# Reading the eight remainder rows of an adjacency matrix in halves, sixteen lanes instead of eight

## What is computed

```python
neighbors = adj @ h                                  # 5000 x 5000 times 5000 x 64
neighbors = neighbors / (num_neighbors[:, None] + 1e-7)
out = concatenate([h, neighbors], axis=-1) @ fc_w.T + fc_b
return x + relu(out)
```

## Time and profile before

| | |
|---|---|
| median of 3 runs | 246.63 us (246.61 to 246.72) |
| the profiled execution: its time, its span | 246.69 us, 245.2 us |
| mean granted TensorE clock | 0.97 |
| busy: PE, DVE, ACT, POOL | 86%, 17%, 6%, 2% |
| chain that ended last: DMA, PE, issue, DVE | 60%, 25%, 11%, 2% |
| moved | 102.79 MB, mean 419 GB/s over the span |
| transfers from SP's queue (q1), from ACT's queue (q10) | 102.37 MB, 0.28 MB |

### The profile page before, as it was taken

The page is one execution under the profiler, slowest core; times in us unless marked ns, Lnnn a source line. Parts: engine busy times, 40 slices in busy tenths (PEclk is TensorE's granted clock), DMA queues, the critical chain, the costliest instruction groups (busy, mean ns, idle before and its releaser), DMA issues.

```text
span 245.2 us, 2432 instructions
## 1 busy us (share of the span) xinstructions
PE 209.9 (86%) x1084; PEld 86.4 (35%) x1084; DVE 41.2 (17%) x101; ACT 15.1 (6%) x34; POOL 4.3 (2%) x14
## 2 busy tenths in 40 slices
PE   0268989797879987999999899898896999788995
PEld 0143344342323432353433234242232233133663
DVE  1762033304400200032000530221000000002301
ACT  2130011101200110010000300000000000000000
POOL 6000000000000000000000000000000000000000
PEclk9999999999979997979999999999997999999999
DMA  8999999999999999999999999999999999999995
GB/s 305 409 428 448 434 424 429 435 434 430 415 435 434 428 428 424 428 428 418 434 445 433 433 425 419 439 428 433 420 444 428 404 428 428 416 421 418 419 404 239
DMA packets 6807, 102.79 MB, mean 419 GB/s; under 512 B 1266, under 2 KB 1870, under 8 KB 3598
## 3 DMA queue, kind: packets, MB, share of 16 engines
q1 hardware_dynamic: 6304, 102.37, 98.2%
q10 hardware_dynamic: 494, 0.28, 0.4%
HBM read 101.37 MB, written 1.28 MB: 419 GB/s over the span
## 4 chain that ended last, share of the span: by engine, by line
DMA 60%; PE 25%; issue 11%; DVE 2%; SPq 1%; DVEq 0%
DMA raw<-adj_group 60%; PE acc L611 21%; DVE rnn_diag L460 2%; PE turned L611 1%; PE y L572 1%; PE y L577 1%; PE y L597 1%; SPq L264 1%; SPq L255 0%; PE y L589 0%; PE turned L560 0%; DVE out_sb L523 0%; DVE rnn_diag L468 0%; PE acc L659 0%; DVE rnn_diag L465 0%
## 5 line engine op out<-in xcount | busy, mean ns | idle before, releaser
L611 PE MATMUL acc<-raw,g_sb 128*64 128x512 f32 (+1 forms) x780 | 163.9, 576 | 19.6 <-DMA raw<-adj_group 19.6
L611 PEld LDWEIGHTS acc<-raw,g_sb 128*64 128x64 f32 x780 | 57.1, 142 | 121.4 <-issue 89.7
L611 PE MATMUL turned<-raw,g_sb 128*64 128x196 f32 x156 | 15.4, 341 | 1.0 <-DMA raw<-adj_group 0.9
L439 DVE TENSOR_TENSOR out_sb<-y,bias 128x128 f32<-128x128 f32 x20 | 4.4, 283 | 53.4 <-ACT g_sb L352 53.4
L572 PE MATMUL y<-w_both,ht 128*128 128x256 f32 (+1 forms) x40 | 12.1, 441 | 0.8 <-ACT ht L346 0.8
L489 DVE TENSOR_TENSOR sums<-acc,rnn_bc 128x512 f32<-128x512 f32 x4 | 2.6, 685 | 60.1 <-PE acc L611 58.1
L611 PEld LDWEIGHTS turned<-raw,g_sb 128*64 128x64 f32 x156 | 10.1, 134 | 6.4 <-DMA raw<-adj_group 4.1
L572 PEld LDWEIGHTS y<-w_both,ht 128*128 128x128 f32 x40 | 8.0, 217 | 3.9 <-issue 2.7
L560 PE MATMUL turned<-ident,h_pairs 128*128 128x128 f32 x20 | 3.7, 315 | 4.5 <-DVE h_pairs L427 4.5
L415 DVE TENSOR_REDUCE var<-sums 128x8 f32<-128x512 f32 x5 | 3.4, 686 | 23.1 <-ACT sums L328 23.1
L515 DVE TENSOR_TENSOR out_sb<-y,out_sb 128x512 f32<-128x512 f32 (+1 forms) x5 | 3.2, 638 | 23.5 <-PE y L643 20.3
(11 more groups left out here) (57 smaller groups left out, 44.7 us busy)
## 6 DMA issues: line engine op xcount, KB each, us to landing
raw<-adj_group SPq DMA_DIRECT2D x9, 5120.0 KB, 27.0
raw<-adj_group SPq DMA_DIRECT2D x7, 4096.0 KB, 28.0
raw<-adj_group SPq DMA_DIRECT2D x4, 2048.0 KB, 29.2
raw<-adj_group SPq DMA_DIRECT2D x7, 784.0 KB, 26.2
raw<-adj_group SPq DMA_DIRECT2D x1, 3840.0 KB, 22.8
raw<-adj_group SPq DMA_DIRECT2D x3, 1024.0 KB, 25.0
raw<-adj_group SPq DMA_DIRECT2D x4, 392.0 KB, 18.9
x_sb<-x SPq DMA_DIRECT2D x2, 576.0 KB, 4.6
```

The source lines that it names most:

```text
L439: last = nc.vector.tensor_tensor(to[:, 2 * k:2 * k + 2, :], weighed_parts(k, 0)[:, :, s, :], bias[:].unsqueeze(1).to_broadcast([LANES, 2, ...
L611: last = nc.tensor.matmul(acc[b][s * HALF:(s + 1) * HALF, 0:width], g_sb[:, t, :], k, start=g < G - 1 and t == 0, stop=t == CH - 1, tile_p ...
```

## The change

The eight rows are read in halves: half h of row r goes to lane 16r + 8h (sixteen lanes, eight apart), each half as one contiguous piece, and one transfer serves a column group. The left halves need the remainder's g on lanes 0, 16, ..., 112, the right halves on lanes 8, 24, ..., 120; the second is a new tile `g_rem`, made by one more matmul into the free tile `turned` and one more ACT copy. In `remainder`, a side that crosses the middle of a group is cut into two matmuls.

```diff
-REM_STEP = 4
-REM_GAP = 8
+REM_STEP = 8
...
-        adj_rem = sb("adj_rem", [LANES, WIDEST, BLOCK + REM_GAP])
+        adj_rem = sb("adj_rem", [LANES, max(WIDTH) // 2])
...
-        ht_rem = sb("ht_rem", [LANES, LANES])
+        ht_rem = sb("ht_rem", [LANES, REM_STEP + LANES])
+        g_rem = sb("g_rem", [LANES, F])
...
-                rows = adj_groups[g][REM0:N, 0:w]
-                lanes = slice(0, REM * REM_STEP, REM_STEP)
-                k = w // (2 * BLOCK) * 2
-                act.dma_start(adj_rem[lanes, 0:k, 0:BLOCK],
-                              rows[:, 0:k * BLOCK].rearrange("r (k c) -> r k c", k=k)).then_inc(rem_loaded, 16)
-                if w > k * BLOCK:
-                    act.dma_start(halves(adj_rem[lanes, k, :])[:, :, 0:BLOCK // 2],
-                                  rows[:, k * BLOCK:w].rearrange("r (s c) -> r s c", s=2)).then_inc(rem_loaded, 16)
+                lanes = slice(0, 2 * REM * REM_STEP, REM_STEP)
+
+                act.dma_start(adj_rem[lanes, 0:w // 2], adj_groups[g][REM0:N, :].rearrange("r (h c) -> (r h) c", h=2)
+                              ).then_inc(rem_loaded, 16)
                 if g == 1:
                     act.wait_ge(rem_cleared, 3)
-                    act.dma_start(adj_rem_last[lanes, 0:2 * SIDE], adj_groups[G - 1][REM0:N, :]).then_inc(rem_last_loaded, 16)
+                    act.dma_start(adj_rem_last[lanes, 0:SIDE],
+                                  adj_groups[G - 1][REM0:N, :].rearrange("r (h c) -> (r h) c", h=2)
+                                  ).then_inc(rem_last_loaded, 16)
...
+                if b == SETS - 1:
+                    nc.scalar.activation(g_rem[:], turned[:, 0:F], ACT.Copy)
...
+                        if i < TAIL_RUN:
+                            h = ht_rows[F:LANES, i:REM0 - TAIL0:TAIL_RUN]
+                        else:
+                            h = ht_rem[F:LANES, REM_STEP:REM_STEP + LANES]
...
+                if apart:
+
+                    last = nc.tensor.matmul(turned[:, 0:F], ht_rem[F:LANES, 0:LANES], w_both[F:LANES, 1, F:2 * F],
+                                            start=True, stop=True)
...
+                half = WIDTH[g] // 2
+                weights = [g_sb[:, CH, :], g_rem[:]]
+                if g == G - 1:
+                    pe.wait_ge(rem_last_loaded, 16)
+                    for s in range(2):
+                        for h in range(2):
+                            last = nc.tensor.matmul(acc[LAST][s * HALF:(s + 1) * HALF, h * SIDE // 2:(h + 1) * SIDE // 2],
+                                                    weights[h], side_columns(adj_rem_last[:, 0:half])[:, s, :, :],
+                                                    start=h == 0, stop=False, tile_position=(0, s * HALF))
                 else:
...
+                    pe.wait_ge(rem_loaded, 16 * (g + 1))
+                    for b in banks(g):
+                        for s, c0, width in sides(g, b):
+
+                            for h in range(c0 // half, (c0 + width - 1) // half + 1):
+                                a, z = max(c0, h * half), min(c0 + width, (h + 1) * half)
+                                last = nc.tensor.matmul(acc[b][s * HALF:(s + 1) * HALF, a - c0:z - c0], weights[h],
+                                                        adj_rem[:, a - h * half:z - h * half],
+                                                        start=False, stop=False, tile_position=(0, s * HALF))
```

More of the change, by code:

```diff
@@ L70, in gnn_layer @@
     WIDTH = [v.shape[1] for v in adj_groups]
-    WIDEST = max(WIDTH) // BLOCK
     def banks(g):
@@ L112, in gnn_layer @@
     LN_OPS = 8
-    REM_LOADS = [sum(1 + (w % (2 * BLOCK) > 0) for w in WIDTH[:g + 1]) for g in range(G - 1)]
     with ExitStack() as ctx:
@@ L343, in copy_turned @@
                     nc.scalar.activation(
-                        ht_rem[HALF:LANES, 0:REM * REM_STEP].rearrange("k (p t z) -> k p t z", t=RUN, z=REM_STEP)[:, :, :, 0],
+                        ht_rem[HALF:LANES, REM_STEP:(2 * REM + 1) * REM_STEP].rearrange(
+                            "k (p t z) -> k p t z", t=RUN, z=2 * REM_STEP)[:, :, :, 0],
                         k[:, LAST_LANES - REM // RUN:LAST_LANES, :], ACT.Copy)
@@ L574, in weigh @@
                     if apart:
-                        h = ht_rows[F:LANES, i:REM0 - TAIL0:TAIL_RUN] if i < TAIL_RUN else ht_rem[F:LANES, :]
+                        if i < TAIL_RUN:
+                            h = ht_rows[F:LANES, i:REM0 - TAIL0:TAIL_RUN]
+                        else:
+                            h = ht_rem[F:LANES, REM_STEP:REM_STEP + LANES]
                         last = nc.tensor.matmul(weighed_tiles(i)[:, w:4 * F], h, w_both[F:LANES, 1, F:2 * F],
                                                 start=True, stop=True)
+                if apart:
+                    last = nc.tensor.matmul(turned[:, 0:F], ht_rem[F:LANES, 0:LANES], w_both[F:LANES, 1, F:2 * F],
+                                            start=True, stop=True)
                 last.then_inc(weighed, 1)
@@ L616, in remainder @@
             def remainder(g):
-                if g < G - 1:
-                    pe.wait_ge(rem_loaded, 16 * REM_LOADS[g])
-                else:
[L621 to L631, removed]
+                half = WIDTH[g] // 2
[7 more added lines that the diff above has]
+                                                    start=h == 0, stop=False, tile_position=(0, s * HALF))
+                else:
+                    pe.wait_ge(rem_loaded, 16 * (g + 1))
[6 more added lines that the diff above has]
+                                                        start=False, stop=False, tile_position=(0, s * HALF))
                 last.then_inc(rem_used, 1)
```

## The result

| | before | changed |
|---|---|---|
| median of 15 runs | 246.63 us (246.41 to 246.82) | 247.12 us (246.82 to 247.43) |
| ratio, with its 95% interval | | 1.0020 (1.0013 to 1.0027) |
| span of the profiled execution | 245.2 us | 245.4 us |

The forecast was 246.35 us, 0.28 us faster. It came out 0.49 us slower, just at the bound of what this kernel's measurement tells from no change, and above the range's 247.0. The profiled execution of the changed kernel took 246.88 us, one of its fastest, so its rows show less than the whole loss: 0.19 us above the 246.69 us of the profiled execution before.

A forecast was written before the change was run, and what follows sets the result against it. Sixteen full DMA engines were taken to bound the kernel, the slowest setting the end. Its lag falling from 2.7 to 2.42 us gave 246.69 - 0.28 = 246.41, less 0.06 for the median: 246.35 us, range 246.0 to 247.0.

The forecast's parts named there:

- The bound: Whole run: the slowest of sixteen full DMA engines plus a fixed tail sets the time; added PE, ACT, POOL work hidden.
- The count of engines: Remainder transfers: eight lanes used eight engines, sixteen lanes would use sixteen, a half row of 10.0 KB each.
- The shape: Marks of one load at 202 us: would span about 2.0 us instead of 2.7, another engine now being last.
- the fetches: Instruction blocks fetched by DMA engines: each taken to hold one engine back 1.5 us, explaining the lags at 202 us.
- 0.42 us on every engine: Remainder transfers after the change: every engine pays 0.42 us; eight engines gain 0.45, the other eight lose 0.42.
- the total work is the same: Remainder transfers: the change only shifts engine time from eight engines to the other eight, leaving the sum unchanged.
- the prediction's own sum: Load at 202 us: last engine at 2.0 + 0.42 = 2.42 instead of 2.7, so 0.28 us earlier.
- The first rival: Remainder transfers: writing lanes another engine fills for raw delays the owner 0.42 to 0.84 us; 246.8 to 247.2 us, chance 0.22.
- The sign named for it: Around 57 to 70 us: ACT's queue share well above 1.7% with fewer packets would show slow foreign lanes.
- The page: SBUF ports: lanes 0, 8, ..., 120 fall on eight ports, two each; bytes at the busiest port stay the same.

The follow-up runs named there:

- matmuls_only: The changed kernel with the old transfers (whole rows to eight lanes), its new matmuls and ACT copy kept: 246.50 us, ratio 1.0001 (0.9992 to 1.0010).
- the added transfers: The kernel before plus sixteen additional transfers on ACT's queue into an unread spare tile, lanes varied: 249.00 us on lanes 0 to 28, 254.18 on sixteen eight apart.
- quarters: The changed kernel with groups 0 and 1's remainder rows in quarters on 32 lanes four apart, four weight tiles: 246.46 us, ratio 0.9994 (0.9985 to 1.0003).
- seven apart in the kernel itself: The changed kernel with its sixteen lanes seven apart from lane 3, all else kept: 247.17 us, ratio 1.0023 (1.0014 to 1.0033).
- the table: Times of the kernel before with sixteen additional transfers, one line per lane choice; sixteen lanes seven apart: 253.01 us, 6.5 above before.

## Why the prediction was wrong

- *The bound* was right: sixteen full engines set the end, and everything else in the change is hidden. matmuls_only shows it within its interval of 0.2 us either way, and the ACT copy took 224 ns where 0.25 us was taken, the POOL memset 1167 ns.
- *The count of engines* was right: eight before, sixteen after, by the marks.
- *The shape* was right by the spread of the marks, which went from 2.7 to 1.95 us. This does not test the missing term: first and last mark both came 0.5 us later than forecast, and the difference between them stayed. Whether the last engine is now one that had been at 2.0 is not shown, as marks name no engine; nor that the fetches made those lags.
- *The step that failed* is the term "0.42 us on every engine", with "the total work is the same". It priced a packet by its engine's time alone and put the delay of raw's own packets at nothing. In the trace of the changed kernel raw's packets took 0.56 us an engine longer, in the mean, in the two stretches with remainder transfers, and the mean mark at 202 us came 0.56 us later. By the added transfers a half row eight apart costs 0.47 to 0.49 us for 4 KB where its own time is 0.15, so for the 10 KB of a half row (2.44 times as much) 1.15 to 1.2 us instead of 0.42. Put into the prediction's own sum, the last engine stands at 2.0 + 1.2 = 3.2 instead of 2.7 us: 0.5 us slower; measured 0.49. That it meets the figure so closely is in part luck, since the 2.0 is the prediction's assumption about which engine has a fetch and no remainder, and in the profiled execution last mark and time both came only 0.2 us later. The same sum gives for quarters, at 0.20 us for 4 KB, 2.0 + 0.49 or the old remainder engines' 2.7 - 0.87 + 0.49 = 2.3, so 2.49, 0.2 us faster, and the interval of quarters (0.37 faster to 0.07 slower) holds it, as it holds no change.
- *The first rival* had mechanism, price (0.42 to 0.84 us on top, against 0.56 in the mean) and result, 246.8 to 247.2 us. It had a chance of 0.22 with the remark that no row spoke against it. For a term that no row showed, this was too little, and the range ended inside the rival's own span. The sign named for it was the wrong one too: ACT's share, "well above 1.7%", came to 2.0% where it had been 1.8, while the delay stood in the bytes of SP's queue.
- *The page* beside that rival, the Trainium skill (SBUF — State Buffer, Door 1: The DMA port swizzle), counts ports: seven apart reach fifteen, eight apart eight. The runs differ (6.5 against 7.6 us for sixteen transfers) by much less than such a count suggests. The Trainium skill (DMA: Bandwidth & Descriptors, The descriptor swizzle) says which engine writes which lanes in a transfer over 128 lanes; by it the lanes 0 to 28 are engine 0 to 7's own and 64 to 92 are not. That the first cost 2.4 and the second 5.9 us agrees, if the eight engines at work are the same in both, which no record shows.

Open: how exactly the lanes are shared out was inferred from costs, no record names an engine. And seven apart in the kernel itself (0.59 us above before) costs more than the table's 0.41 us a transfer would make it (2.0 + 1.0 - 2.7 = 0.3): that lies just outside its interval, 0.35 to 0.81 us.

## What to carry to other kernels

Where all DMA engines are full, splitting a small transfer over more of them can gain only if its lanes are chosen so that each engine keeps writing those that it fills for the main stream. Here even that came out level with not splitting (ratio 0.9985 to 1.0003). Otherwise the main stream's own packets get longer, and the loss appears as fewer bytes of the main stream in the same busy share, not in the small transfer's row. Price such a transfer by repeating it a dozen times on a queue with nothing behind it; a 0.2% question becomes a 2% one. And count marks in narrow windows: they show how far the last engine is behind the others, before and after a change.

## Not expected of the hardware

- Eight engines by the marks, the same 32 KB a transfer beside full raw traffic: 0.15 us on lanes 0, 4, ..., 28, 0.37 us on lanes 64, 68, ..., 92.
- Beside such packets raw's own packets of 32768 bytes get longer, from 1219 to 1259 ns in the mean (145 to 236 us), while the small ones take 159 and 165 ns in the median.
- Sixteen engines, the same 64 KB: 0.20 us on lanes 0, 4, ..., 124, 0.49 us on lanes 0, 8, ..., 120, 0.74 us on lanes 0 to 15.
- One block of instructions (16 KB) held one engine's share of a load back by 1.1 to 1.7 us. That the eight such fetches of this program decide which engine ends last was assumed, not shown.
